# Delta stage: a level's cast moved ahead of the second chunk, value weights' low parts one turn later, filter taps scaled on ScalarE

## What is computed

```python
mixed = einsum('bsh,ch->bcs', x, Wqkv)          # 8192 channels
z = einsum('bsh,vh->bsv', x, Wz)
mixed = silu(causal_depthwise_conv(mixed, conv_w))   # four taps
q, k, v = split(mixed); q, k = l2norm(q) / sqrt(DK), l2norm(k)
def step(state, q_t, k_t, v_t, g_t, b_t):       # one head
    state = state * exp(g_t)
    delta = (v_t - state^T k_t) * b_t
    state = state + k_t delta^T
    return state, state^T q_t
core = scan(step)
core = core * rsqrt(mean(core^2) + EPS) * norm_w * silu(z)
x = layernorm(x + einsum('bsv,hv->bsh', core, Wout))
```

## Time and profile before

| | |
|---|---|
| median of three runs | 3586.7 us |
| profiled execution, its own time | 3586.82 us |
| its span | 3585.1 us |
| busy: TensorE, VectorE, ScalarE, GpSimd | 3102.5, 2647.0, 2138.8, 1523.1 us |
| delta stage | about 765 to 3260 us of the span |

### The profile page before, as it was taken

The page is one execution under the profiler, slowest core; times in us unless marked ns, Lnnn a source line. Parts: engine busy times, 40 slices in busy tenths (PEclk is TensorE's granted clock), DMA queues, the critical chain, the costliest instruction groups (busy, mean ns, idle before and its releaser), DMA issues. The chain is left out here.

```text
span 3585.1 us, 82199 instructions
## 1 busy us (share of the span) xinstructions
PE 3102.5 (87%) x29261; PEld 2175.7 (61%) x29280; DVE 2647.0 (74%) x4821; ACT 2138.8 (60%) x5429; POOL 1523.1 (42%) x1853
## 2 busy tenths in 40 slices
PE   6999788267999999999999999999999999983185
PEld 4666565244676666766767667676666766762042
DVE  3444389865887878878788787787877878766875
ACT  4444400146776767767777777677776777763553
POOL 1111277125554655545555455454554555530000
PEclk9999999678999999999999999999999999996698
DMA  4000011001100011000110101101010010101201
GB/s 188 13 13 1 9 43 41 19 22 49 31 25 31 19 43 32 25 32 19 43 32 21 35 19 43 32 19 37 19 43 32 20 37 19 43 7 47 94 1 47
DMA packets 43229, 120.67 MB, mean 34 GB/s; under 512 B 5824, under 2 KB 10048, under 8 KB 39488
## 3 DMA queue, kind: packets, MB, share of 16 engines
q1 hardware_dynamic: 42816, 115.30, 10.3%
HBM read 110.75 MB, written 4.54 MB: 32 GB/s over the span
## 5 line engine op out<-in xcount | busy, mean ns | idle before, releaser
L2012 DVE TENSOR_TENSOR delta_Pb<-delta_bank,delta_lev 128x512 f16<-128x512 f32 x448 | 311.1, 694 | 210.5 <-PE delta_bank L2345 210.5
L2004 DVE SCALAR_TENSOR_TENSOR delta_F<-delta_bank,delta_cw,delta_F 128x510 f32<-128x510 f32 (+1 forms) x512 | 381.3, 745 | 67.6 <-ACT delta_far L1823 55.4
L1590 POOL TENSOR_SCALAR_AFFINE_SELECT delta_LA<-delta_LA 128x512 f32<-128x512 f32 x128 | 81.6, 637 | 817.0 <-DVE delta_LA L2041 807.9
L2319 PE MATMUL delta_bank<-delta_xh,delta_qkvh 128*128 128x512 f16 x1024 | 390.7, 382 | 4.5 <-DVE delta_qkvl L1972 3.0
L2319 PE MATMUL delta_bank<-delta_xl,delta_qkvh 128*128 128x512 f16 x1024 | 390.4, 381 | 0.0
L2319 PE MATMUL delta_bank<-delta_xh,delta_qkvl 128*128 128x512 f16 x1024 | 390.2, 381 | 0.0
L1610 POOL TENSOR_TENSOR delta_F<-delta_F,delta_far 128x506 f32<-128x506 f32 x256 | 278.3, 1087 | 203.4 <-DVE delta_F L2004 203.4
L1817 ACT ACTIVATE delta_F<-delta_bank,delta_cw 128x512 f32<-128x512 f32 x256 | 178.7, 698 | 269.9 <-PE delta_bank L2319 268.6
L1782 ACT ACTIVATE delta_Xi<-delta_bank 128x512 f16<-128x512 f32 x320 | 190.0, 594 | 182.5 <-PE delta_bank L2360 179.0
L2029 DVE CAST delta_XT<-delta_bank 128x512 f16<-128x512 f32 x384 | 262.9, 685 | 38.8 <-PE delta_bank L2364 38.6
L2304 PE MATMUL delta_bank<-delta_zh,delta_xh 128*128 128x256 f16 x1024 | 280.1, 274 | 0.6 <-ACT delta_gz L1845 0.6
(11 more groups left out here) (353 smaller groups left out, 9404.4 us busy)
## 6 DMA issues: line engine op xcount, KB each, us to landing
delta_Gb<-g_rows SPq DMA_DIRECT2D x66, 512.0 KB, 5.4
delta_st_qkv<-in_Wqkv SPq DMA_DIRECT2D x17, 1024.0 KB, 8.6
conv_T<-filters SPq DMA_DIRECT2D x32, 256.0 KB, 3.1
delta_st_zo<-in_Wz SPq DMA_DIRECT2D x16, 512.0 KB, 9.0
delta_st_zo<-in_Wout SPq DMA_DIRECT2D x16, 512.0 KB, 6.3
ffn_ahead_W<-in_W SPq DMA_DIRECT2D x2, 4096.0 KB, 17.1
conv_ahead_C<-in_ctx_rev SPq DMA_DIRECT2D x1, 6144.0 KB, 27.5
attn_xt<-in_xT SPq DMA_DIRECT2D x8, 512.0 KB, 4.5
```

Of the source, the lines that this page charges most:

```text
L2004: ve.scalar_tensor_tensor(dst, src, cw_tap(i, 3 - lag), dst, ALU.mult, ALU.add)\
L2012: ve.tensor_tensor(left(Pb[:, lvl, :, :], lvl), comp(bank[5], lvl), bc(lev[:, lvl, :].rearrange("p (n s) -> p n s", s=1 << lvl), 1, 8), AL ...
L2319: ins = te.matmul(bk[:, :], ww[:, QKV[job], kc, :], xx[:, kc, tok:tok + 512], start=(m == 0), stop=(m == 11))
```

## The change

Four edits, all in the delta stage. (1) VectorE's `level_xt(1, 1)` moves from behind `level_p(2, 1)` to ahead of `second_chunk`. (2) The low parts of the two value weights leave the turn with `it.u(2) == 3` and open the next one (`value_weights`, `it.u(1) == 3`). (3) The taps are scaled by ScalarE instead of VectorE (`next_conv`), behind its last high part, and for the first key head before its first. (4) The last two instructions of `newton` become one, and the counter `rn` has 3 events.

```diff
--- before.py
+++ after.py
@@ -1378,7 +1378,7 @@
             s=3, la=8, dg=2, lt=2, ll=2, vt=2, v=2, v16=1,
             pa=7, px=5, pd=6, pm=7, xc=5, xt=7, xir=1, xti=1,
             sv=7, u0=2, r=2, w=2, t16=1, t2=1, o=2,
-            so=8, rr=1, lr=1, rn0=1, rn=4, ogs=8, og=2, ct=2, ch=2, cl=2,
+            so=8, rr=1, lr=1, rn0=1, rn=3, ogs=8, og=2, ct=2, ch=2, cl=2,
         ).items():
             g[name] = counter(name, per)
         g_load = [counter(f"g_load{i}", 1, 16) for i in range(2)]
@@ -1709,6 +1709,11 @@
                 act.wait_ge(pro["gs"].sem, pro["gs"].at(q + 1))
                 if q % 2:
                     act.sem_inc(pro["rows"].sem, 1)
+            def conv_weights(kh):
+                act.wait_ge(w_load["c"].sem, w_load["c"].at(1, kh))
+                sc.activation(cw[:, :], st_c[:, :], ACT.Copy, scale=CS).then_inc(w_c.sem, 1)
+
+            conv_weights(0)
             for name in ("qkv", "z"):
                 for c in range(CHUNKS[name]):
                     high(name, c, 0)
@@ -1757,7 +1762,7 @@
 
                     if not it.has(-1):
                         return
-                    after("rn", 4, -1)
+                    after("rn", 3, -1)
                     after("ct", 2, -2)
                     for c in range(2):
                         for q in (2 * b_, 2 * b_ + 1):
@@ -1858,6 +1863,13 @@
                     if it.u(2) == 3 and it.has(2):
                         after("qj", 1 + c, 2)
                         high("qkv", c, it.kh(2) + 1)
+
+                def next_conv():
+
+                    if it.u(2) == 3 and it.has(2):
+                        after("taps", 8, 2)
+                        after("far", 4, 2)
+                        conv_weights(it.kh(2) + 1)
 
                 def next_z(c):
                     if it.u(0) == 3 and it.has(0) and it.has(1):
@@ -1904,6 +1916,7 @@
                 sc.preload_act_table_set("natural_log_exp_and_others")
                 key_norm()
                 next_qkv(3)
+                next_conv()
                 next_z(0)
                 next_z(1)
                 decays(0, 2)
@@ -1972,11 +1985,6 @@
                 ve.scalar_tensor_tensor(chunk(name, c, 2), chunk(name, c, 0), split_scale(name), chunk(name, c, 1),
                                         ALU.mult, ALU.subtract).then_inc(w_lo[name].sem, 1)
 
-            def conv_weights(kh):
-                dve.wait_ge(w_load["c"].sem, w_load["c"].at(1, kh))
-                ve.tensor_scalar(cw[:, :], st_c[:, :], CS, None, ALU.mult).then_inc(w_c.sem, 1)
-
-            conv_weights(0)
             for name in ("qkv", "z"):
                 for c in range(CHUNKS[name]):
                     low(name, c, 0)
@@ -2078,9 +2086,8 @@
                     ve.scalar_tensor_tensor(lr[:, :], lr[:, :], -0.5, rr[:, :], ALU.mult, ALU.mult)\
                         .then_inc(g["rn"].sem, 1)
                     after("rn", 2, -1)
-                    ve.tensor_scalar(lr[:, :], lr[:, :], 1.5, None, ALU.add).then_inc(g["rn"].sem, 1)
-                    after("rn", 3, -1)
-                    ve.tensor_tensor(rn[:, :], rn[:, :], lr[:, :], ALU.mult).then_inc(g["rn"].sem, 1)
+                    ve.scalar_tensor_tensor(rn[:, :], lr[:, :], 1.5, rn[:, :], ALU.add, ALU.mult)\
+                        .then_inc(g["rn"].sem, 1)
 
                 def residual(k):
 
@@ -2148,11 +2155,10 @@
                     if it.u(2) == 3 and it.has(2):
                         low("qkv", c, it.kh(2) + 1)
 
-                def next_conv():
-                    if it.u(2) == 3 and it.has(2):
-                        after("taps", 8, 2)
-                        after("far", 4, 2)
-                        conv_weights(it.kh(2) + 1)
+                def value_weights(c):
+
+                    if it.u(1) == 3 and it.has(1):
+                        low("qkv", c, it.kh(1) + 1)
 
                 def next_z(c):
                     if it.u(0) == 3 and it.has(0) and it.has(1):
@@ -2162,6 +2168,8 @@
                     if it.u(-1) == 0 and it.has(-1):
                         low("o", c, it.kh(-1))
 
+                value_weights(2)
+                value_weights(3)
                 level_p(4, 0)
                 add_out(2, -2)
                 decayed_j0(0)
@@ -2188,21 +2196,18 @@
                 refined(0)
                 query_norm()
                 next_o(1)
+                level_xt(1, 1)
                 second_chunk()
                 conv_lag("v1", 1, 2)
                 level_p(2, 1)
-                level_xt(1, 1)
                 next_qkv(0)
                 next_qkv(1)
                 residual(1)
                 level_xt(2, 1)
                 key_norm()
-                next_conv()
-                next_qkv(2)
                 level_p(3, 1)
                 refined(1)
                 add_out(0, -1)
-                next_qkv(3)
                 next_z(0)
                 next_z(1)
                 add_out(1, -1)
```

## The result

The changed kernel takes **3529.4 us** (median of four runs, 3529.15 to 3529.42). The kernel before, run four times beside it on the same chip, takes 3587.4 (3585.93 to 3590.93). The ratio is 0.9836, with a 95% interval from 0.9822 to 0.9851: 1.6% faster. The forecast was 3534.5. The profiled execution took 3529.42 us, its span 3527.7; before they were 3586.82 and 3585.1, so the two traces differ by 57.4 us.

A forecast was written before the change was run, and what follows sets the result against it. TensorE, 97% busy at full clock, was taken as the bound, so only its waits could be gained. Ordinary turns 27.0 plus heavy turns 25.3 gave 52.3 us: 3586.8 - 52.3 = 3534.5 us, range 3521 to 3562.

The forecast's parts named there:

- the rival in which GpSimd is no obstacle: Heavy turn: GpSimd doesn't hold VectorE's low parts; 2.03 us gained there, 59.5 in all, 3527.3 us; chance 0.08.
- Ordinary turns, 0.60 forecast: Cast of level 1 in VectorE's idle time before V: L2360 starts 0.60 us earlier in 45 turns, 27.0 us.
- with the same 0.15 us behind it the start is 2009.45: Ordinary turn: L2360 starts 0.15 us after Pb's end at 2009.30, instead of at 2010.05.
- The slower rival: Early cast pushes V by 0.60 us, t is held by GpSimd, L2360 0.85 later: 3613.5 us; chance 0.03.
- Heavy turn, 1.58 forecast: Turn splitting the next weights, once per key head: 1.44 + 0.14 us less before L2313, 16 times, 25.3 us.
- The three readings in it: Heavy turn: Pb 0.14 us after the reciprocal; first low part held by GpSimd's far tap; L2313's idle about 0.4 us.
- The term 1.44 us: Heavy turn: without taps' scaling and one value weight's low part, Pb starts 1.44 us sooner after the reciprocal.
- the push that I had put into the range: Heavy turn: only 0.39 us idle before V, so the cast pushes V at most 0.2 us, 3 us over 16 turns.
- The edits at nothing: Value weights at the next turn's start (1 us of cover), taps' scaling on ScalarE, Newton's merged step: 0 us each.
- Signs of being wrong: In the profile after: V later against the matmuls of L2470, Xi releasing TensorE, or longer waits for t.

The follow-up runs named there:

- e8: The changed kernel with the cast of level 1 between t and the two filter taps instead of ahead of the second chunk: 3568.0 us, ratio 0.9940.
- e1: The kernel before with only the cast of level 1 moved ahead of the second chunk: 3551.3 us, ratio 0.9900.
- e3: The changed kernel with the scaling of the filter taps back on VectorE, between key norm and Pb: 3539.9 us, ratio 0.9866.
- e11: The changed kernel with the value weights' low parts back in the heavy turn, around the first addition to X: 3550.2 us, ratio 0.9888.
- e5: The changed kernel with the low part of k moved behind the first addition to X: 3522.5 us, ratio 0.9814.
- e10: The changed kernel with Newton's last two steps as two instructions again: 3533.1 us, ratio 0.9841.
- e4: The changed kernel with GpSimd's float16 copy of V moved behind its far tap of v1: 3519.0 us, ratio 0.9811.
- e9: The changed kernel with GpSimd's copy of V behind its far tap and k's low part behind the first addition to X: 3504.5 us, ratio 0.9762.

## Why the prediction was right

The sum was 52.3 us and the traces give 57.4. Both mechanisms are the forecast's; both terms were a little small. The number alone would not show it: 3529.4 lies nearer to the rival in which GpSimd is no obstacle (3527.3) than to the forecast (3534.5). What decides between them is the heavy turn.

**Ordinary turns, 0.60 forecast, 0.67 measured.** The step that was off is "with the same 0.15 us behind it the start is 2009.45". The 0.15 us were taken from the start of L2360 behind XT. Behind Pb, L2365 starts 0.08 us after the end of it, in step with TensorE's row. So Pb costs no wait, and the gain is the whole of the old one: 45 x 0.67 = 30.2 instead of 27.0. V was left where it was, as forecast (0.28 us to spare). e8 shows what this rests on: with the same cast 0.60 us behind V, 38.6 us are lost. The slower rival needed the cast to push V; in the ordinary turns it never did.

**Heavy turn, 1.58 forecast, 1.65 measured.** The three readings in it hold. With both instructions gone Pb follows the reciprocal 0.10 us from start to start (forecast 0.14), where it was 1.58 before. The low parts collide with the far tap as worked out (1.88 us for the pair). TensorE's wait for X is 0.34 us where 0.4 was forecast. 16 x 1.65 = 26.4 instead of 25.3. The rival in which GpSimd is no obstacle (2.03 us) is refuted by the 1.88 us of the pair, in e1, e3 and e11 as well, and by e5: with one of the two low parts moved away, 6.9 us more are gained. The Trainium skill (SBUF — State Buffer, Who interferes with whom) says that a VectorE instruction with two inputs in SBUF contends with a GpSimd instruction that reads SBUF, and that the order in which they issue decides who is blocked. The traces agree in that the low part is held when GpSimd's is under way (1.27 to 1.28 us against 0.67 to 0.68). Waiting and then running in full would be 0.68 us after GpSimd's end, however; measured are some 0.55.

The term 1.44 us came out right partly by luck. It was read from where the reciprocal and Pb stood, with the scaling at 0.80 and the low part at 0.68, as rows of before have them, and GpSimd's Ll (1972.90 to 1975.18 there), which runs beside them, is not in the prediction at all. e3 and e11 show that 0.80 and 0.68 are not the two instructions' own costs: the scaling costs 0.67 us in the turn and the low part about 1.2, each with the other gone, because either one takes GpSimd's hold. The sum for both gone holds only because Pb, which comes next, is not held; nothing in the prediction asked whether it would be. Each alone would have been forecast wrong, and for e11 it was.

In this turn the cast comes directly ahead of V with no idle time left, the push that I had put into the range with up to 3 us. V starts 1.38 us behind the start of the output weights' low part, where it was 1.25. It cost nothing: t, right behind V, is held by GpSimd in either case, and from the start of that low part to the end of t it is 2.96 us before and after (1941.77 to 1944.73 here).

**The edits at nothing.** The value weights keep 1.07 us of cover (forecast 1). The scaling on ScalarE takes 0.20 us, hidden. Newton's step gives nothing (e10). All three are as forecast; the first two are worth what they take away from VectorE's chain in the heavy turn: 20.8 us (e11) and 10.5 us (e3) when put back one at a time. These two can't be added: they overlap in the hold.

**Signs of being wrong.** Two of those that I named came up in small: Xi as a releaser of TensorE (1.0 us in two waits in its first turns) and a longer wait for t (10.8 us against 10.4). Neither touches the steady turns' account.

**What is left.** 45 x 0.67 + 16 x 1.65 = 56.6 of 57.4 us. Against that stand five ordinary turns of before, 36.56 us long instead of 36.94, which have no like in the changed kernel (0.38 us less gain in each, 1.9 in all). In them GpSimd's copy of V started only when t was over. VectorE and GpSimd of the kernel before, an ordinary turn of the common kind and one of these five:
```profile
1143.38 0.92 DVE L2109 CAST delta_t<-delta_V 128x512 f16<-128x512 f32 x1
...
1180.34 0.52 DVE L2109 CAST delta_t<-delta_V 128x512 f16<-128x512 f32 x1
```
```profile
1143.41 0.61 POOL L1653 CAST delta_V<-delta_V 128x512 f16<-128x512 f32 x1
...
1180.86 0.61 POOL L1653 CAST delta_V<-delta_V 128x512 f16<-128x512 f32 x1
```
Side by side t takes 0.92 us, ahead of the copy 0.52. e4 made this the rule. The rest, 57.4 - 56.6 + 1.9 = 2.7 us, stays open. Where to look: from the first reciprocal to the last the changed kernel is 53.0 us shorter, ahead of the first it is 1.0 us longer, and behind the last 5.4 us shorter, where the last four turns of the stage stand.

## What to carry to other kernels

A cast or copy that is late only by its place in a queue belongs in the idle time of its engine just before an instruction which waits for someone else. Look at what stands behind the place as well, buffers that come free included. Before costing an instruction by its row, see whether the row's end goes with another engine's end: then it is a hold, and when the instruction leaves, the next one can inherit it (the low part did, Pb did not). Two edits that shorten the same queue are to be tested each alone and both together.

## What the runs showed of the hardware

- VectorE held by GpSimd: an instruction of 0.68 us with two inputs in SBUF, started beside a GpSimd tensor-tensor, ended 0.54 to 0.56 us after it, in five places (before at 1958.68, the change at 1946.69, e1 at 1953.97, e9 at 1936.62, e11 at 1959.06). One that started together with a GpSimd copy (before at 1975.12) was not held and took 0.68; the copy took 1.31 us instead of 0.76.
- A small instruction is held as well, from SBUF to SBUF with one input: scaling 128x16 took 0.17 us by itself and 0.59 to 0.95 beside GpSimd's Ll (before and e1).
- A cast of 128x512 from SBUF to SBUF took 0.43 us by itself (e4) and 0.87 to 0.92 beside GpSimd's cast or its operation on EL (before at 1143.38, the change, e4 at 1936.22). The Trainium skill (SBUF — State Buffer, Who interferes with whom) names cast and tensor_scalar among the operations that can contend with GpSimd. These two kinds did here.
- GpSimd pays too: its copy of V took 0.61 us alone and 1.07 beside VectorE's low part (e4, e9); its pair of Ll took 2.27 us in e9 and 2.71 beside the second low part in e4.
- There is no one delay from the end of a VectorE instruction to the start of the matmul that waits for it: 0.06 us from t to L2460 (all 54 waits of the change), 0.24 from the taps to L2318 (most ordinary turns of before, the change and e8), 0.15 from the cast to L2360 (before). The 0.08 from Pb to L2365 is an upper bound, since TensorE's own row allowed no earlier start.
